# Index columns copied for one or for two ring groups at a time in the plain gather passes of a graph-network kernel

## The chip, the core and the metric

The kernel runs on one core of a Trainium2 chip. The time is the device time of one execution in microseconds (us); before the change it was 10801.46 us, the median of three runs.

## The reference, cut to what matters

A graph of 6250 nodes (256 features each) and 100000 edges, sorted by destination, passes through four layers: `L0` an attention layer with four heads, `L1` a convolution with a weight for each edge, `L2` two convolutions one behind the other, `L3` an attention layer with eight heads. Each is added to the residual stream. What matters here are the three sums over edges of `L1` and `L2`:

```python
# L1
out = segment_sum(w[:, None] * support[col], row, n) + segment_sum(w[:, None] * support[row], col, n)
# L2, twice
msg = x[src] @ W_msg + b_msg
agg = segment_sum(msg, dst, num_segments=n)
return agg + x @ W_self + b_self
```

For each of them the row `table[src]` of 256 floats must be fetched for every edge and added to the row of its destination.

## The kernel before, in words

The edges are padded to 784 tiles of 128 (`ET`). Nodes are kept in 49 tiles of 128 (`NT`). Four edge tiles are a *ring group* (`EG` = 4), so there are 196 groups (`NEG`). Two edge tiles are a pair. One *visit* joins one pair with one node tile; there are 440 visits (`NV`, 392 pairs and 48 for pairs that straddle node tiles), taken in 110 units of four (`VG`, `NU`).

`plain_pass` (L1016) sums the edges of one layer. It is called three times: `l1` (L2205; weighted, with a `fold` that adds eight partial sums of the other direction, which an earlier pass scattered to HBM), `l2a` (L2229) and `l2b` (L2256), the last two with an `own` matrix product for each node tile in between. Within a pass the engines work side by side:

- GpSimd (POOL in the profile) runs `gather` (L1003). For each group it waits for the group's slot in the ring (L1008, L1009; `RG` = 6 slots of four tiles in `rows_in`), copies the group's four index columns out of `gidx` into the slot of `gather_rows` (L998, in `index_columns`), waits for the copy's own semaphore (L999, L1000), and issues four indirect DMAs (L1012), each of which fetches 128 rows of 1 KB. The loop's body is one turn of the ring, six groups; 32 turns run in the loop, and four groups follow it.
- The sync engine (SP) runs `landed_groups` (L967): it waits until the four DMAs of a group have landed and raises `s_landed` (L976); three groups later it gives the slot back (`ring_free`, L984) when `s_add` shows that all visits of that group are done.
- VectorE (DVE) builds one-hot matrices `hot` for the eight half-visits of a unit from `iota` and `rel`: in `l2a` and `l2b` by one instruction of 128x1024 with two inputs (L941), in `l1` by eight small ones (L944). It also adds each visit's result from PSUM to the accumulator (L956).
- TensorE waits for `s_landed` (L1100) and for a free PSUM bank (L1101), and multiplies the one-hots with the fetched rows (L1103), a visit being two products of 128x128 by 128x256. Each fp32 product stands in the trace as two records.
- In `l2a` and `l2b` TensorE also transposes a node tile (L1111) and multiplies it with the layer's own weights (L1119), once in two units; ScalarE copies for it.

`gather` is also called by the two attention layers: `attention_fetch0` (L1256; groups of four, ring of eight) and `attention_fetch3` (L1902; groups of eight tiles, `GS` = 8, ring of six). Between the gathers no engine but GpSimd issues indirect DMAs. `scatter_pass` (L1722) is an earlier phase. The helper `turns` (L63) takes the number of steps and the number of steps in one loop body; a step's `u.c` is a Python number that counts within the body, `u.val` is the edge group's number (in the loop a register expression).

Of the kernel before, what the change touches and what calls it, by code (L numbers as in the profile page):

```python
# [5 lines left out]
I32 = mybir.dt.int32  # L6
# [4 lines left out]
P = 128  # L11
N, D, E = (6250, 256, 100000)
# [3 lines left out]
ET = 784  # L16
# [9 lines left out]
GS = 2 * VG  # L26
EG = 4
NEG = ET // EG
RG, RG0 = (6, 8)
# [33 lines left out]
def turns(eng, total, body, lag, steady=None):  # L63
    first = -(-lag // body) * body
    loops = max(0, ((steady or total) - first) // body)
    if loops < 2:
        first, loops = total + lag, 0
    for v in range(first):
        yield Turn(v, v, total, False)
    if loops:  # L70
        with eng.Fori(0, loops) as i:
            for k in range(body):
                yield Turn(i * body + (first + k), first + k, total, True)
        for v in range(first + loops * body, total + lag):
            yield Turn(v, v, total, False)

def build(nc, t, out):
    with ExitStack() as top:
        made = {}

        def own(name):
            made[name] = made.get(name, 0) + 1
            return name if made[name] == 1 else f'{name}_{made[name]}'

        def sb(name, shape, dt=F32, ctx=top):
            return ctx.enter_context(nc.sbuf_tensor(own(name), shape, dt))

        def bank(name, ctx):
            return ctx.enter_context(nc.psum_tensor(own(name), [P, 512], F32))

        def sem(name):
            return top.enter_context(nc.semaphore(name))
# [18 lines left out]
        gidx = sb('gidx', [P, ET], I32)  # L111
# [13 lines left out]
        def dram(name, shape, dt=F32):  # L125
            return nc.dram_tensor(name, shape, dt).ap()
        T0, T1, T2, T3 = (dram(f'table{i}', [NP, D]) for i in range(4))
        T4 = dram('table4', [NP, WT])
# [15 lines left out]
        own_v, own_a, own_p = (sem(f's_own_{k}') for k in 'vap')  # L144
# [19 lines left out]
        ring_free = [sem(f's_ring_free{b}') for b in range(RG0)]  # L164
# [22 lines left out]
        def phase():  # L187
            return nc.Block()
# [757 lines left out]
        def rows_count(name, n=2):  # L946
            return [Count(sem(f's_rows_{name}{b}')) for b in range(n)]
# [45 lines left out]
                sp.wait_ge(ring_free[b], 1)  # L993
                sp.sem_inc(ring_free[b], -1)

        def index_columns(g, u, ring, per, idx):
            b = u.c % ring
            g.tensor_copy(idx[:, b, :], gidx[:, bass.ds(u.val * per, per)]).then_inc(own_p, 1)  # L998
            g.wait_ge(own_p, 1)  # L999
            g.sem_inc(own_p, -1)  # L1000
            return [idx[:, b, j:j + 1] for j in range(per)]

        def gather(g, table, rows_of, s_rows, ring, per, free, idx):  # L1003
            top_row = g.to_reg(NP - 1)

            def fetch(u):
                b = u.c % ring
                g.wait_ge(free[b], 1)  # L1008
                g.sem_inc(free[b], -1)  # L1009
                rows = index_columns(g, u, ring, per, idx)  # L1010
                for j in range(per):
                    g.indirect_dma_start(out=rows_of(b * per + j), out_offset=None, in_=table, in_offset=bass.IndirectOffsetOnAxis(ap=rows[j], axis=0), bounds_check=top_row, oob_is_err=True).then_inc(s_rows[b].sem, 16)  # L1012
            for t_ in turns(g, ET // per, ring, 0):
                fetch(t_.at(0))

        def plain_pass(name, table, acc, acc_flat, width, weighted, fold=None, own=None):  # L1016
            NB = 4
            s_rows = rows_count(name, RG)
            with ExitStack() as ctx:
                G = sb('rows_in', [P, RG * EG, width], F32, ctx)  # L1020
                idx = sb('gather_rows', [P, RG, EG], I32, ctx)
                hot = sb('hot', [P, 2, GS, P], F32, ctx)
                wgt = sb('step_weights', [P, S], F32, ctx) if weighted else None
                ps = [bank(f'ps_p{i}', ctx) for i in range(NB)]
# [13 lines left out]
                with phase() as block:  # L1038
# [45 lines left out]

                    @block.gpsimd
                    def _(g):
                        gather(g, table, lambda k: G[:, k, 0:D], s_rows, RG, EG, ring_free, idx)

                    @block.tensor
                    def _(te):  # L1090
# [130 lines left out]
        def attention_fetch0(LG, attc, room):  # L1221
            G = part(room, 0, [RG0 * EG, D])
            rows_by = part(room, RG0 * EG * D, [2, GS * P // 2]).bitcast(BF16)
            spread = part(room, RG0 * EG * D + GS * P, [2, GS * P])
            s_rows = rows_count('att0_', RG0)
# [2 lines left out]
            row_free = [sem(f's_row_free{b}') for b in (0, 1)]  # L1228
            with ExitStack() as ctx:
                feat = sb('feat', [P, 2, 2 * D], F32, ctx)  # L1230
                idx = sb('gather_rows', [P, RG0, EG], I32, ctx)
                featT = sb('featT', [P, 2, 4, P], F32, ctx)
                psX = [bank(f'psX{b}', ctx) for b in (0, 1)]
                psF = [bank(f'psF{b}', ctx) for b in (0, 1)]
# [1 line left out]
                with phase() as block:  # L1236
# [16 lines left out]

                    @block.gpsimd
                    def _(g):
                        gather(g, T0, lambda k: G[:, k, :], s_rows, RG0, EG, ring_free, idx)  # L1256

                    @block.scalar
                    def _(a):
# [595 lines left out]
        def attention_fetch3(LG, SV, rows_room, T_room):  # L1855
            R3 = 6
            NG3 = ET // GS
            AHEAD = 13
            G = part(rows_room, 0, [R3 * GS, WT])
            rows_by = part(T_room, 0, [2, GS * P // 2]).bitcast(BF16)  # L1860
            spread = part(T_room, 2 * GS * P, [2, GS * P])
            s_rows = rows_count('att3_', R3)
# [3 lines left out]
            free3 = [sem(f's_slot_free3{b}') for b in range(R3)]  # L1866
            read3 = [sem(f's_slot_read3{b}') for b in range(R3)]
            with ExitStack() as ctx:
                psS = [bank(f'psS{b}', ctx) for b in (0, 1)]
                idx = sb('gather_rows', [P, R3, GS], I32, ctx)  # L1870
                with phase() as block:

                    @block.sync
# [25 lines left out]

                    @block.gpsimd  # L1900
                    def _(g):
                        gather(g, T4, lambda k: G[:, k, :], s_rows, R3, GS, free3, idx)  # L1902

                    @block.scalar
                    def _(a):
# [460 lines left out]
```

## Time and profile before

| what | value |
|---|---|
| median of the three runs | 10801.46 us (10778.44 to 10802.27) |
| time of the profiled execution | 10752.12 us |
| its span in the trace | 10750.4 us |
| TensorE's mean granted clock | 0.739 |
| busy: TensorE matmul, weight load | 6331.9 us (59%), 4941.0 us (46%) |
| busy: VectorE, ScalarE | 5005.6 us (47%), 1331.9 us (12%) |
| busy: GpSimd | 5855.2 us (54%), 5805 instructions |
| software queue of the DMA engines (all gathers and scatters) | 634.04 MB, 26.7% of 16 engines |

The shares are averages over some forty phases with different limits, so they don't say what bounds a plain pass. The three plain passes lie at about 4530 to 5720 us, 5783 to 7030 us and 7142 to 8390 us of the span. "POOLq", "SPq", "PEq" and "DVEq" are the sequencers of the engines, which take instructions in order and hand them to the engine; a line behind the arrow names what an idle engine was waiting for, and "issue" is time in which it waited for nothing that the profile shows.

### The profile page before, as it was taken

Reading aid. Unit: us, or ns where it says so; the run is one execution under the profiler, and the core shown is the slowest. Engines: PE = TensorE matmul, PEld = TensorE weight load, DVE = VectorE, ACT = ScalarE, POOL = GpSimd, SP = SyncE. Lnnn points to the kernel's source line nnn. Section 1 sums busy time; section 2 is a strip of 40 time slices with the busy share of each in tenths; the row PEclk is TensorE's granted clock in tenths of the full one; section 3 lists DMA queues with packets and bytes.
Section 4 is the critical chain, followed back from the end, with each engine's and each line's share of the span. In section 5 each row is a group of like instructions: output and inputs, shape, how many; then the busy total and the mean of one; then the engine's idle time right before and its main releaser. Section 6 shows DMA issues by size and latency. Waiting matters only on the chain. (4 is left out here: it accounts for less than half of the span.)

```text
span 10750.4 us, 137753 instructions
## 1 busy us (share of the span) xinstructions
PE 6331.9 (59%) x24674; PEld 4941.0 (46%) x24675; DVE 5005.6 (47%) x12212; ACT 1331.9 (12%) x3940; POOL 5855.2 (54%) x5805
## 2 busy tenths in 40 slices
PE   4888875757466666555554555555555642222575
PEld 2888864546344444433333444444444442222454
DVE  6555558885444444355553222242222321114888
ACT  2222211213222222100001000010000300000000
POOL 3777740000288888777775777747777167763000
PEclk9898878988777777676766777677777655555798
DMA  4666674541377777644433222222222166663454
GB/s 147 189 190 187 186 231 152 169 136 35 69 104 105 104 104 105 111 134 137 133 117 91 82 82 82 82 75 81 83 83 83 41 193 204 201 193 99 129 170 155
DMA packets 835068, 1358.92 MB, mean 126 GB/s; under 512 B 112279, under 2 KB 488661, under 8 KB 834981
## 3 DMA queue, kind: packets, MB, share of 16 engines
q0 software_dynamic: 315328, 634.04, 26.7%
q1 hardware_dynamic: 385684, 562.46, 16.0%
q10 hardware_dynamic: 133968, 161.50, 4.8%
q8 instruction: 26, 0.43, 0.0%
q14 instruction: 62, 0.50, 0.0%
HBM read 943.05 MB, written 414.50 MB: 126 GB/s over the span
## 5 line engine op out<-in xcount | busy, mean ns | idle before, releaser
L1012 POOL DMA_INDIRECT rows_in<-table,gather_rows x2352 | 2500.5, 1063 | 1034.2 <-issue 511.1
L1103 PE MATMUL ps_p<-rows_in,hot 128*128 x5280 | 2000.5, 542 | 1584.6 <-SPq L976 1328.8
L1103 PEld LDWEIGHTS ps_p<-rows_in,hot 128*128 128x128 f32 x5280 | 1360.3, 271 | 2180.1 <-issue 1928.7
L1722 POOL DMA_INDIRECT scatter_sums<-regionC,idx x880 | 1387.3, 1576 | 307.1 <-issue 246.0
L956 DVE TENSOR_TENSOR regionC<-regionC,ps_p 128x257 f32 (+2 forms) x1320 | 558.6, 423 | 1767.9 <-DVEq L953 1569.1
L1464 PE MATMUL ps_p<-regionA 128*128 128x265 f32 (+1 forms) x3520 | 969.4, 435 | 426.0 <-DVE regionC L956 194.4
L1464 PEld LDWEIGHTS ps_p<-regionA 128*128 128x128 f32 x3520 | 735.3, 214 | 659.8 <-DVE regionC L956 239.3
L1012 POOL DMA_INDIRECT regionB<-table,gather_rows x784 | 848.4, 1082 | 344.5 <-issue 272.2
L1012 POOL DMA_INDIRECT regionC<-table,gather_rows x784 | 817.1, 1042 | 296.7 <-issue 265.1
L1927 PE MATMUL psS<-dst_scores,regionA 128*128 x1760 | 393.4, 362 | 793.7 <-issue 385.4
L1927 PEld LDWEIGHTS psS<-dst_scores,regionA 128*128 128x128 f32 x1760 | 383.7, 330 | 803.4 <-issue 803.4
L1795 PE MATMUL psC<-regionC 128*128 128x128 f32 x1760 | 370.5, 377 | 649.1 <-PEq L1793 647.8
L1807 PE MATMUL psO<-regionA,regionC 128*128 x1760 | 675.1, 552 | 8.8 <-PEq L1806 1.8
L1795 PEld LDWEIGHTS psC<-regionC 128*128 128x128 f32 x1760 | 319.2, 272 | 753.3 <-issue 752.9
L956 DVE TENSOR_TENSOR regionB<-regionB,ps_p 128x265 f32 (+1 forms) x880 | 372.5, 423 | 586.1 <-DVEq L953 472.5
L1537 POOL MEMSET ones<- 128x128 f32 x2 | 0.4, 206 | 1109.1 <-POOLq L2052 940.3
L1807 PEld LDWEIGHTS psO<-regionA,regionC 128*128 128x128 f32 x1760 | 495.1, 295 | 120.7 <-issue 23.8
L1496 DVE TENSOR_TENSOR regionA<-regionA,logits 128x512 f32<-128x512 f32 x880 | 547.6, 684 | 0.0
L1317 PEld LDWEIGHTS psL<-att_cols,featT 128*128 128x128 f32 x3520 | 526.0, 215 | 37.6 <-issue 4.9
L1292 PE MATMUL psX<-regionA,regionB 128*128 x1760 | 528.7, 429 | 21.7 <-PEq L1288 18.6
L1369 DVE TENSOR_TENSOR feat<-regionB,psX 128x512 f32<-128x512 f32 x440 | 301.8, 686 | 499.5 <-DVEq L1368 375.0
L998 POOL COPY gather_rows<-gidx 128x4 int32 (+1 forms) x882 | 221.4, 251 | 468.1 <-POOLq L1009 461.8
(303 smaller groups left out, 8011.7 us busy)
## 6 DMA issues: line engine op xcount, KB each, us to landing
regionA<-edge_rows SPq DMA_DIRECT2D x880, 256.0 KB, 3.2
edge_rows<-regionB SPq DMA_DIRECT2D x196, 512.0 KB
edge_rows<-regionC SPq DMA_DIRECT2D x392, 256.0 KB
regionC<-srcrow_d SPq DMA_DIRECT2D x220, 256.0 KB
scatter_sums<-zero_rows ACTq DMA_DIRECT2D x8, 6400.0 KB, 42.3
regionA<-scatter_sums ACTq DMA_DIRECT2D x49, 1024.0 KB
rows_in<-table,gather_rows POOLq DMA_INDIRECT x2352
regionB<-rrow_d ACTq DMA_DIRECT2D x110, 256.0 KB
```

Source lines behind the costliest of these rows:

```text
L956: v.tensor_tensor(dst_, dst_, ps[(u.c * VG + j) % nbank][:, 0:width], ALU.add).then_inc(s_add.sem, 1)
L1012: g.indirect_dma_start(out=rows_of(b * per + j), out_offset=None, in_=table, in_offset=bass.IndirectOffsetOnAxis(ap=rows[j], axis=0), boun ...
L1103: x = te.matmul(ps[(u.c * VG + j) % NB][:, 0:width], hot[:, b, 2 * j + k, :], at_tile(G, slot[j] * 2 + k), start=k == 0, stop=k == 1)
L1292: x = te.matmul(psX[b][:, k * D:(k + 1) * D], spread[:, ub, at:at + P], at_tile(A256, nt), start=True, stop=True)
L1317: x = te.matmul(psL[gb][:, col:col + HEADS0], featT[:, b, 2 * k + c, :], attc[:, c, :], start=c == 0, stop=c == 1)
L1369: v.tensor_tensor(feat[:, b, :], G[:, bass.ds(slot * 2, 2), :].rearrange('p a c -> p (a c)'), psX[b][:, :], ALU.add).then_inc(own_v, 1)
L1464: x = te.matmul(ps[(u.c * VG + j) % NB][:, 0:width], hot[:, b, 2 * j + k, :], Gs[:, b * GS + 2 * j + k, :], start=k == 0, stop=k == 1)
L1496: v.tensor_tensor(o, i, w, ALU.mult).then_inc(aux_full[b], 1)
L1722: g.indirect_dma_start(out=scat, out_offset=bass.IndirectOffsetOnAxis(ap=idx[:, b, j:j + 1], axis=0), in_=sums[:, b, j, :], in_offset=None ...
L1795: x = te.matmul(psC[b][:, j * P:(j + 1) * P], hot[:, b * Q + j, :], same[:, b * Q + j, :], start=True, stop=True)
L1807: x = te.matmul(psO[2 * b + j // 2][:, j % 2 * D:(j % 2 + 1) * D], pairs[:, b * Q + j, :], at_tile(SUP, nt[j // 2]), start=True, stop=True)
L1927: x = te.matmul(psS[b][:, j * HEADS3:(j + 1) * HEADS3], spread[:, b, j * P:(j + 1) * P], at_tile(SV, nt[j // 2]), start=True, stop=True)
```

## The change

`index_columns` gets a number `together`. With 2, it copies the index columns of two groups (eight columns) at every second group, and nothing at the other; with 1 it does what it did. The plain passes use 2, the attention layers 1. The buffer `gather_rows` of a plain pass grows from 24 to 48 columns, two turns of the ring, and the body of the gather loop from six to twelve groups (16 turns in the loop, four groups behind it). In the attention layers only the buffer's shape is written differently.

```diff
-        def index_columns(g, u, ring, per, idx):
-            b = u.c % ring
-            g.tensor_copy(idx[:, b, :], gidx[:, bass.ds(u.val * per, per)]).then_inc(own_p, 1)
-            g.wait_ge(own_p, 1)
-            g.sem_inc(own_p, -1)
-            return [idx[:, b, j:j + 1] for j in range(per)]
-
-        def gather(g, table, rows_of, s_rows, ring, per, free, idx):
+        def index_columns(g, u, ring, per, idx, together):
+            b, at = (u.c % (together * ring), u.c % together)
+            if at == 0:
+                n = together * per if not isinstance(u.val, int) else min(together * per, ET - u.val * per)
+                g.tensor_copy(idx[:, b * per:b * per + n], gidx[:, bass.ds(u.val * per, n)]).then_inc(own_p, 1)
+                g.wait_ge(own_p, 1)
+                g.sem_inc(own_p, -1)
+            return [idx[:, b * per + j:b * per + j + 1] for j in range(per)]
+
+        def gather(g, table, rows_of, s_rows, ring, per, free, idx, together):
             top_row = g.to_reg(NP - 1)
 
             def fetch(u):
                 b = u.c % ring
                 g.wait_ge(free[b], 1)
                 g.sem_inc(free[b], -1)
-                rows = index_columns(g, u, ring, per, idx)
+                rows = index_columns(g, u, ring, per, idx, together)
...
-            for t_ in turns(g, ET // per, ring, 0):
+            for t_ in turns(g, ET // per, together * ring, 0):
                 fetch(t_.at(0))
...
-                idx = sb('gather_rows', [P, RG, EG], I32, ctx)
+                idx = sb('gather_rows', [P, 2 * RG * EG], I32, ctx)
...
-                        gather(g, table, lambda k: G[:, k, 0:D], s_rows, RG, EG, ring_free, idx)
+                        gather(g, table, lambda k: G[:, k, 0:D], s_rows, RG, EG, ring_free, idx, 2)
...
-                idx = sb('gather_rows', [P, RG0, EG], I32, ctx)
+                idx = sb('gather_rows', [P, RG0 * EG], I32, ctx)
...
-                        gather(g, T0, lambda k: G[:, k, :], s_rows, RG0, EG, ring_free, idx)
+                        gather(g, T0, lambda k: G[:, k, :], s_rows, RG0, EG, ring_free, idx, 1)
...
-                idx = sb('gather_rows', [P, R3, GS], I32, ctx)
+                idx = sb('gather_rows', [P, R3 * GS], I32, ctx)
...
-                        gather(g, T4, lambda k: G[:, k, :], s_rows, R3, GS, free3, idx)
+                        gather(g, T4, lambda k: G[:, k, :], s_rows, R3, GS, free3, idx, 1)
```

## Rows read from the trace of the kernel before

**Rows 1.** The page's costliest groups: busy, mean ns | idle before, releaser.

```profile
L1012 POOL DMA_INDIRECT rows_in<-table,gather_rows x2352 | 2500.5, 1063 | 1034.2 <-issue 511.1
L1103 PE MATMUL ps_p<-rows_in,hot 128*128 x5280 | 2000.5, 542 | 1584.6 <-SPq L976 1328.8
```

**Rows 2.** Waits of the second pass: engine line <- releaser: us, times, longest us.

```profile
PE ps_p L1103 <- SPq L976: 479.4, 174, 4.9
POOL rows_in L1012 <- issue: 157.2, 468, 1.8
POOL rows_in L1012 <- POOLq L1000: 129.0, 162, 0.8
POOL gather_rows L998 <- POOLq L1009: 63.0, 1, 63.0
POOL rows_in L1012 <- POOLq L1009: 39.6, 130, 0.3
```

**Rows 3.** The three passes, busy by engine, granted clock, DMA share, GB/s.

```profile
core 0: us, PE busy (x) PEld busy (x) DVE busy (x) ACT busy (x) POOL busy (x), PEclk, DMA share, GB/s
4530.00:5720.00 1190.00, 676.21 (x1752) 463.28 (x1752) 626.76 (x1416) 0.00 (x0) 842.68 (x980) 0.69 0.43 129
5782.00:7030.00 1248.00, 736.56 (x2046) 518.00 (x2046) 343.68 (x598) 38.64 (x97) 900.86 (x980) 0.72 0.28 82
7142.00:8390.00 1248.00, 729.99 (x2046) 520.03 (x2046) 342.07 (x598) 38.62 (x97) 900.85 (x980) 0.73 0.28 82
```

**Rows 4.** Timeline of GpSimd in the first pass: start, us, what, idle before.

```profile
4594.57 1.01 POOL L1012 DMA_INDIRECT rows_in<-table,gather_rows  x1 [0.30 <-issue]
4595.89 1.01 POOL L1012 DMA_INDIRECT rows_in<-table,gather_rows  x1 [0.30 <-issue]
4596.91 0.19 POOL L998 COPY gather_rows<-gidx 128x4 int32 x1
4597.90 1.04 POOL L1012 DMA_INDIRECT rows_in<-table,gather_rows  x1 [0.79 <-POOL gather_rows L998]
4599.24 1.01 POOL L1012 DMA_INDIRECT rows_in<-table,gather_rows  x1 [0.30 <-issue]
4600.56 1.01 POOL L1012 DMA_INDIRECT rows_in<-table,gather_rows  x1 [0.31 <-issue]
4601.88 1.01 POOL L1012 DMA_INDIRECT rows_in<-table,gather_rows  x1 [0.30 <-issue]
4602.90 0.19 POOL L998 COPY gather_rows<-gidx 128x4 int32 x1
```

**Rows 5.** Timeline of GpSimd in `attention_fetch3`: groups of eight gathers.

```profile
9003.33 1.04 POOL L1012 DMA_INDIRECT regionC<-table,gather_rows  x1 [0.80 <-POOL gather_rows L998]
...
9012.58 1.01 POOL L1012 DMA_INDIRECT regionC<-table,gather_rows  x1 [0.30 <-issue]
9016.88 0.19 POOL L998 COPY gather_rows<-gidx 128x8 int32 x1 [3.28 <-POOLq L1009]
```

**Rows 6.** GpSimd by shape: first pass, then the second.

```profile
L1012 POOL DMA_INDIRECT rows_in<-table,gather_rows x784 | 802.2, 1023 | 345.0 <-issue 191.9 <-POOLq L1000 69.9 <-POOL gather_rows L998 47.6
L998 POOL COPY gather_rows<-gidx 128x4 int32 x192 | 39.8, 207 | 13.4 <-POOLq L1009 12.2
...
L1012 POOL DMA_INDIRECT rows_in<-table,gather_rows x784 | 850.3, 1085 | 345.0 <-issue 157.2 <-POOLq L1000 129.0 <-POOLq L1009 39.6
L998 POOL COPY gather_rows<-gidx 128x4 int32 x192 | 49.9, 260 | 64.1 <-POOLq L1009 63.0
```

**Rows 7.** Timeline of the second pass: a one-hot of VectorE beside the gathers.

```profile
6290.82 1.22 DVE L941 TENSOR_TENSOR hot<-iota,rel 128x1024 f32<-128x1024 f32 x1
6290.96 1.96 POOL L1012 DMA_INDIRECT rows_in<-table,gather_rows  x1 [0.30 <-issue]
...
6304.91 0.20 POOL L998 COPY gather_rows<-gidx 128x4 int32 x1
...
6306.98 3.79 PE L1103 MATMUL ps_p<-rows_in,hot 128*128 x8 [3.94 <-SPq L976]
```

**Rows 8.** VectorE in the second pass by shape: the one-hots.

```profile
L941 DVE TENSOR_TENSOR hot<-iota,rel 128x1024 f32<-128x1024 f32 x110 | 134.5, 1224 | 5.4 <-DVEq L961 0.2
```

**Rows 9.** Timeline of GpSimd: long pauses, two in the first pass, one in `attention_fetch3`.

```profile
4702.68 1.01 POOL L1012 DMA_INDIRECT rows_in<-table,gather_rows  x1 [1.76 <-issue]
4848.68 1.01 POOL L1012 DMA_INDIRECT rows_in<-table,gather_rows  x1 [1.77 <-issue]
...
9148.27 1.07 POOL L1012 DMA_INDIRECT regionC<-table,gather_rows  x1 [1.40 <-issue]
```

## The prediction

> **What bounds the kernel now.** The page's busy shares decide nothing here, so I first read the costliest groups. In the plain passes TensorE's products stand idle for 1584.6 us, 1328.8 of them until the sync engine says that a group of gathered rows has landed (L976) [rows 1]. GpSimd's gathers of the same passes wait mostly for "issue", for nothing another engine does. Next I read the waits of one pass. TensorE waits 174 times for a landing, 479.4 us together; GpSimd waits for a slot of the ring (L1009) once for long, 63.0 us ahead of the pass, and after that never longer than the 0.3 us that lies ahead of every gather [rows 2]. So nobody holds GpSimd up, and it holds up the others. The windows agree: TensorE is busy for 676 of 1190 us in the first pass and for 737 and 730 of 1248 in the others, the DMA engines for 28% to 43% [rows 3]. Last I read GpSimd's timeline: gather behind gather without a hole that belongs to someone else [rows 4]. A plain pass lasts as long as GpSimd needs to issue 784 gathers and 196 copies, and a microsecond saved there is a microsecond of the kernel, three times over.
>
> **The change, part by part.**
>
> *Copies removed.* 196 copies a pass become 98, each for eight columns; over three passes 294 go. What one costs must be read from start to start. Inside a group a gather starts 1.32 us behind the one before (4594.57, 4595.89). Across a copy it is 2.01 us (4595.89 to 4597.90): the gather's 1.01, the copy's 0.19, and then 0.79 in which the next gather can't start, since its sequencer had to wait for the copy's semaphore (L1000) before it could take the gather up [rows 4]. Without the copy the 0.19 and the wait go, and the usual 0.30 stays. The gather behind a copy is also longer itself, 1.04 against 1.01, so the next start comes after 1.34 instead of 1.32 (4597.90, 4599.24). Together 0.69 + 0.02 = 0.71 us for each copy, and 294 x 0.71 = **209 us**. A check: the group's period is 4602.90 - 4596.91 = 5.99 us, and 196 of them are 1174 of the pass's 1190.
>
> By durations alone the sum would be smaller: 294 copies of 0.207 to 0.272 us are some 70 us, and the wait behind them is booked as idle time. The Trainium skill ("Perfetto Trace Analysis", GPSIMD Engine Instruction) advises to time GpSimd by the spacing of starts and calls its spans unreliable; by that rule it is the 209 that counts.
>
> *Is the gap of 0.30 what stays where a group begins without a copy?* There the sequencer still waits for a slot and lowers its semaphore (L1008, L1009). In the trace this work is already hidden: the second gather of a group is put down to L1009 in 130 cases, with 0.3 us at the longest [rows 2], so the sequencer reaches the next group's slot while the present group's first gathers run, some three gathers early. Eight gathers in a row at that pace exist as well: in `attention_fetch3` from 9003.33 to 9012.58, seven spacings, 9.25 us, 1.32 each [rows 5]. The bounds are 0.30 and 0.79 (the gap when the sequencer does stop); I take 0.30.
>
> *The copies that stay are twice as wide.* The eight-column copy takes 0.19 us as the four-column one does [rows 4, 5]. Cost nothing.
>
> *Twice the loop body, twice the buffer.* The body holds 48 gathers instead of 24, and half of the 32 branches of a pass go. `attention_fetch3` runs a loop with 48 gathers in its body at the same spacing [rows 5], so I take nothing; the branch is hidden behind running gathers. The buffer is a few bytes more. The attention layers issue the same instructions as before: nothing.
>
> *One-hots of VectorE against GpSimd.* In the first pass a gather takes 1.023 us on average and a copy 0.207; in the second 1.085 and 0.260 [rows 6]. The excess is 784 x 0.062 + 196 x 0.053 = 59 us a pass. It comes from the 110 one-hots of 1.22 us [rows 8]: a gather that starts under one is held until it ends (1.96 us from 6290.96, under a one-hot from 6290.82) [rows 7]. That is 0.54 us a one-hot. If the starts of gathers fall anywhere under a one-hot, the mean hold is about half its length, 0.6, with copies or without. The same 110 one-hots meet the same 784 gathers afterwards, so I leave the 59 us as they are. The bounds are a hold of 0 and one of 1.22: from 119 us less to 150 us more for both passes. Neither end is near, as the phase of gathers against one-hots wanders with the number of visits in a group; a quarter of it, ±45 us, goes into the range.
>
> Two sentences of the Trainium skill would give something else. By "SBUF — State Buffer" (Who interferes with whom) a VectorE instruction with two SBUF inputs collides with GpSimd instructions that read SBUF, and by "Perfetto Trace Analysis" (DMA Instruction — SWDGE) a DMA that GpSimd issues reads no tensor; only copies would be held, and half of the 59 us would go with half of the copies, 59 more for both passes. The trace doesn't bear the second one out: copies carry only 10 of the 59 us, and a gather itself was held to 1.96 us.
>
> *Do the others keep up?* A group now comes every 5.99 - 0.71/2 = 5.64 us, in the later passes every (1248 - 70)/196, some 6.0. TensorE is busy 737/196 = 3.8 us a group at a mean granted clock of 0.72; all of it at 1.2 GHz would be an estimated 3.8 x 0.72/0.5 = 5.4 us. Even then it keeps up, barely. Slots are given back in time: a group lands about 2 us behind its last gather (6304.91 to 6306.98) [rows 7], the slot behind it is released three groups late, and the ring has six; that leaves more than a group of spare time. What a late slot looks like is seen in `attention_fetch3`, 3.28 us ahead of a copy [rows 5]; the plain passes show none.
>
> *Sum.* -209 us on the path. The profiled execution took 10752.12 us, so its like comes to 10543. It lies 49 us below the median of the runs shown, so against that median: 10801 - 209 = **10592 us**, 1.9% less. A measurement of this kernel can tell about 0.3%, 32 us, from no change.
>
> **The rivals.**
>
> *The sequencer still stops at the group's border.* If the wait for the slot cost what the wait for the copy did, 0.79 would stay and only the copy itself would go: 294 x 0.2 = 59 us, 10742. Against it: the sequencer's lead [rows 2]. Chance 0.03.
>
> *The consumers become the bound.* If TensorE, at the lower clock and with its waits for VectorE's additions, can't take a group in less than about 6.0 us in the stretches with many visits, slots come back late and only half the gain remains: 10697. For it: the estimate of 5.4 lies near 5.64. Against it: in 174 of 196 groups it waited for rows, for 2.8 us each [rows 2]. Chance 0.04.
>
> *It doesn't save what it says.* If landings rather than issues set TensorE's pace, and the DMA engines moved rows no faster for being asked earlier, no change: 10801. Against it: they are busy 28% in the later passes [rows 3]. Chance 0.02.
>
> *Slower: GpSimd's long pauses multiply.* Once in 96 gathers, seven times in the first pass, a gather is preceded by 1.76 us instead of 0.30, with no releaser; in `attention_fetch3` it comes once in 80, at 1.4 [rows 9]. It looks like a store of requests that must be emptied, always ahead of a group's second gather, behind a copy. If the copies' breaks are what lets it empty unseen, half as many breaks could bring a pause with every copy that is left: 294 x 1.46 = 429 us, less the 209: +220, 11021. It decides from 143 pauses more, one in some 14 gathers. Against it: eight gathers in a row bring one in 80, not one in 14. Chance 0.03.
>
> **How the numbers follow.** My forecast has 0.88, with 10592. Its range takes ±45 us for the one-hots, some 20 for the scatter of the medians (24 us between the runs shown) and a little for the gap: 10515 to 10665. The first rival and the consumers' lie above it; they, the third and the slower one are the 0.12 left out. To "faster" go the forecast, the first rival and the second: 0.95. "Same" 0.02, "slower" 0.03.
>
> **What would show it right or wrong.** In the profile after: 294 copies in the plain passes, of eight columns, at about 0.2 us; 588 gaps of 0.79 become 294, and a gather without a copy ahead of it starts 1.32 us behind its neighbour across the group's border; idle time ahead of the gathers falls by 294 x 0.49 = 144 us from 1034.2. The first pass falls from 1190 to 1120 us, the others from 1248 to 1178. TensorE's wait for L976 falls by almost as much as the passes, and POOL's wait for L1009 stays at 0.3. One pause in 80 to 96 gathers remains. It is wrong if a gap of 0.79 stands at borders without a copy, if a wait for L1009 of some microseconds appears ahead of a copy or a gather, or if the passes shorten by much less than GpSimd's saved time.

## The result and the profile after

The changed kernel takes 10647.11 us (median of 4 runs, 10630.78 to 10659.21) against 10797.9 us for the kernel before on the same chip (4 runs, 10778.44 to 10802.27): a ratio of 0.9863 with a 95% interval of 0.9842 to 0.9883, or 151 us less. The forecast was 209 us less, a time of 10592 us with a range of 10515 to 10665. The range holds the result; 0.72 of the gain came. Medians are given with the lowest and highest run or, as a ratio, with their 95% interval; where a kernel ran only once, the text says so.

The profiled execution took 10657.3 us (span 10655.6, mean granted clock 0.738). The lines of the code have moved: the copy is L1000, its wait L1002, the slot's wait L1011, the gather L1014, the product L1105. These are the page's costliest groups again (busy, mean ns | idle before, releaser), the answer to [rows 1]:

```profile
L1014 POOL DMA_INDIRECT rows_in<-table,gather_rows x2352 | 2470.6, 1050 | 944.0 <-issue 693.5
L1105 PE MATMUL ps_p<-rows_in,hot 128*128 x5280 | 1916.0, 524 | 1518.2 <-issue 527.6
```

The idle time ahead of the gathers fell by 90 us (1034.2 to 944.0) where 144 were forecast. Which pass is short of it can be read from the gathers line by line, one row for each pass (durations min/median/max in ns, then the first and the last start). The kernel before:

```profile
L1012 POOL DMA_INDIRECT rows_in<-table,gather_rows x784: 1008/1015/1197, 4531.6 to 5718.5; - x196
L1012 POOL DMA_INDIRECT rows_in<-table,gather_rows x784: 1007/1015/2064, 5783.5 to 7028.4; - x196
L1012 POOL DMA_INDIRECT rows_in<-table,gather_rows x784: 1008/1015/2061, 7143.6 to 8387.9; - x196
L1012 POOL DMA_INDIRECT regionC<-table,gather_rows x784: 1008/1015/1566, 8613.0 to 9791.4; - x196
```

The changed kernel:

```profile
L1014 POOL DMA_INDIRECT rows_in<-table,gather_rows x784: 1006/1012/1194, 4536.9 to 5728.3; - x196
L1014 POOL DMA_INDIRECT rows_in<-table,gather_rows x784: 1006/1012/2085, 5793.6 to 6956.9; - x196
L1014 POOL DMA_INDIRECT rows_in<-table,gather_rows x784: 1006/1012/2067, 7071.7 to 8238.4; - x196
L1014 POOL DMA_INDIRECT regionC<-table,gather_rows x784: 1006/1012/1563, 8463.5 to 9684.8; - x196
```

From first to last start, the second pass went from 1244.9 to 1163.3 us (-81.6) and the third from 1244.3 to 1166.7 (-77.6); 70 each were forecast. The first went from 1186.9 to 1191.4 (+4.5). The three together make -155, close to the 151 between the medians. (The fourth row is `attention_fetch3`, which the change leaves alone. It is 43 us longer in the second of the two profiled executions, most of the reason why their spans differ by only 95.)

On GpSimd's own timeline the change did what it should. Start, us, what, idle before, in the first pass:

```profile
5114.77 1.01 POOL L1014 DMA_INDIRECT rows_in<-table,gather_rows  x1 [0.30 <-issue]
5116.09 1.01 POOL L1014 DMA_INDIRECT rows_in<-table,gather_rows  x1 [0.30 <-issue]
5117.40 1.01 POOL L1014 DMA_INDIRECT rows_in<-table,gather_rows  x1 [0.30 <-issue]
5118.42 0.19 POOL L1000 COPY gather_rows<-gidx 128x8 int32 x1
5119.41 1.04 POOL L1014 DMA_INDIRECT rows_in<-table,gather_rows  x1 [0.79 <-POOL gather_rows L1000]
```

There is no copy between 5108.16 and 5118.42, eight gathers stand 1.32 us apart, and the group's border inside them leaves no mark: the gap there is 0.30. The copy of eight columns takes 0.19, and the 0.79 behind it has stayed, for 98 copies instead of 196. [rows 4] show the same stretch with a copy after every fourth gather.

But in the first pass GpSimd now waits for something else. The waits of the first pass after (engine, line <- releaser: us, times, longest us):

```profile
PE ps_p L1105 <- DVE regionB L956: 262.6, 87, 10.3
PE ps_p L1105 <- SPq L976: 118.2, 16, 48.1
POOL rows_in L1014 <- POOLq L1011: 67.8, 67, 7.3
POOL gather_rows L1000 <- POOLq L1011: 40.7, 10, 12.1
```

And of the same pass before:

```profile
PE ps_p L1103 <- SPq L976: 349.5, 127, 5.6
PE ps_p L1103 <- DVE regionB L956: 22.6, 13, 4.0
POOL rows_in L1012 <- POOLq L1009: 35.7, 117, 0.3
POOL gather_rows L998 <- POOLq L1009: 12.2, 1, 12.2
```

By these rows TensorE no longer waits mostly for rows; it waits for VectorE's additions, 262.6 us instead of 22.6. (How far the split by releaser can be trusted is said behind the experiments.) GpSimd waits for free slots of the ring, up to 7.3 us at a time and 67.8 + 40.7 us together, where the longest wait inside the pass was 0.3. One such place in the changed kernel, all engines, TensorE's weight loads left out:

```profile
5270.94 2.13 DVE L944 TENSOR_SCALAR hot<-iota,rel,step_weights 128x128 f32<-128x128 f32 x8
...
5271.17 2.07 PE L1105 MATMUL ps_p<-rows_in,hot 128*128 x4 [2.36 <-DVE regionB L956]
5272.99 4.01 DVE L1174 TENSOR_REDUCE regionA<-regionA 128x256 f32<-128x2304 f32 x1
5276.92 2.10 DVE L956 TENSOR_TENSOR regionB<-regionB,ps_p 128x256 f32 x4
...
5277.48 2.92 PE L1105 MATMUL ps_p<-rows_in,hot 128*128 x6 [4.24 <-SPq L976]
5278.15 1.01 POOL L1014 DMA_INDIRECT rows_in<-table,gather_rows  x1 [7.33 <-POOLq L1011]
```

VectorE is in the reduction of the sums (4.01 us, L1174) while products finished before wait in the banks. After it four additions run back to back (2.10 us), TensorE starts again, and only then a slot comes free for GpSimd, which has stood for 7.33 us. The kernel before has the same reduction, and its GpSimd never waited over 0.3 us inside the pass. Why does the changed one?

### The profile page after: what moved, and what is told of

Its sections match the earlier page's. It is cut to its first block and busy times, and to the rows that moved or that the text cites. A ratio compares the mean times of both kernels' runs of the same rounds, so it can differ in the third digit from the quotient of the medians.

```text
span 10655.6 us, 136733 instructions
## 1 busy us (share of the span) xinstructions
PE 6231.9 (58%) x24674; PEld 4869.8 (46%) x24675; DVE 5016.8 (47%) x12212; ACT 1330.7 (12%) x3940; POOL 5743.0 (54%) x5511
## 5 line engine op out<-in xcount | busy, mean ns | idle before, releaser
L1014 POOL DMA_INDIRECT rows_in<-table,gather_rows x2352 | 2470.6, 1050 | 944.0 <-issue 693.5
L1105 PE MATMUL ps_p<-rows_in,hot 128*128 x5280 | 1916.0, 524 | 1518.2 <-issue 527.6
L1105 PEld LDWEIGHTS ps_p<-rows_in,hot 128*128 128x128 f32 x5280 | 1312.6, 262 | 2081.5 <-issue 1850.3
L1014 POOL DMA_INDIRECT regionB<-table,gather_rows x784 | 846.1, 1079 | 344.5 <-issue 293.9
L1014 POOL DMA_INDIRECT regionC<-table,gather_rows x784 | 813.0, 1037 | 297.3 <-issue 265.4
L1319 PE MATMUL psL<-att_cols,featT 128*128 128x4 f32 x3520 | 471.4, 257 | 16.6 <-PEq L1312 8.3
```

What stands on the lines that cost most here:

```text
L1105: x = te.matmul(ps[(u.c * VG + j) % NB][:, 0:width], hot[:, b, 2 * j + k, :], at_tile(G, slot[j] * 2 + k), start=k == 0, stop=k == 1)
L1319: x = te.matmul(psL[gb][:, col:col + HEADS0], featT[:, b, 2 * k + c, :], attc[:, c, :], start=c == 0, stop=c == 1)
```

## The experiments

Every kernel here has a mask: the values that TensorE, VectorE and SyncE read from tables and wait for are put through `& 1023` first, which leaves them as they are, since all are smaller. c0_after, c1_after and c2_after are the changed kernel with the mask and nothing else, one for each chip used, and c0_before is the kernel before with it. The mask, its main lines (a third wait, of VectorE in an attention layer, has it too):

```diff
-                                te.wait_ge(s_landed.sem, group[j] + s_landed.base)
+                                te.wait_ge(s_landed.sem, (group[j] & 1023) + s_landed.base)
...
-                done = of_visits(sp, visits_by[0:1, :], u.val, regs, NV)[0]
+                sp.load(regs, visits_by[0:1, bass.ds(u.val, 1)])
+                sp.reg_alu(masked[0], regs[0], 1023, ALU.bitwise_and)
+                done = sp.snap(masked[0], min_val=0, max_val=NV)
```

**The first chip: control, one part undone, two pieces of work made lighter.** e1_fold_single undoes the change in the first plain pass alone:

```diff
-                        gather(g, table, lambda k: G[:, k, 0:D], s_rows, RG, EG, ring_free, idx, 2)
+                        gather(g, table, lambda k: G[:, k, 0:D], s_rows, RG, EG, ring_free, idx, 1 if fold else 2)
```

e2_short_reduce reduces one of the nine partial sums, and e3_small_loads loads one of eight; both leave out part of the sum that the first pass folds in.

```diff
-                                v.tensor_reduce(total, parts[:, b].rearrange('p k c -> p c k'), AX.X, ALU.add).then_inc(own_v, 1)
+                                v.tensor_reduce(total, parts[:, b, 0:1].rearrange('p k c -> p c k'), AX.X, ALU.add).then_inc(own_v, 1)
...
-                                a.dma_start(parts[:, b, 0:CHAINS, :], scat.rearrange('(k n) c -> n k c', k=CHAINS)[bass.ds(u.val * (P // 2), P), :, :]).then_inc(s_load[b].sem, 16)
+                                a.dma_start(parts[:, b, 0:1, :], scat.rearrange('(k n) c -> n k c', k=CHAINS)[bass.ds(u.val * (P // 2), P), 0:1, :]).then_inc(s_load[b].sem, 16)
```

> The changed kernel with one register operation more ahead of three kinds of waits: the value that is loaded from memory is masked with 1023 before it is waited against (L976 to L984 on the sync engine, L1100 on TensorE, the attention layer's wait on VectorE). All experiments below carry these masks, so this run is their control. Both theories: like the changed kernel, 10630 to 10670 us, first plain pass about 1190 us, the second and third about 1165 to 1170 us.

> The first plain pass (the one with the fold) copies index columns for one group again, the other two for two. Theory A (in the first pass something other than GpSimd's issue sets the pace once a group takes less than about 6.05 us, so the 98 copies that are gone there bring nothing): no more than 15 us off the control, the first pass at 1185 to 1195 us. Rival (the first pass did gain and lost it by chance in the profiled execution): about 70 us slower than the control.

> The fold's reduction in the first plain pass reads one of nine partial sums instead of nine (its output leaves the eight scattered sums out); its loads stay. VectorE's 4.0 us become some 0.4, 49 times. Theory B (VectorE's reduction stands in order ahead of the additions that free TensorE's banks, so TensorE and then the ring come late): the first pass falls to about 1120 us, as forecast, and GpSimd waits for slots no more. Theory C (the loads of 1 MB hold the gathers' landings up): the first pass stays at 1180 to 1195 us.

> The fold's loads in the first plain pass fetch one of the eight scattered sums (128 KB instead of 1 MB each); VectorE's reduction stays as long (its output adds seven stale rows). Theory C (the loads hold the landings up): the first pass falls to about 1120 us and a group lands about 2 us behind its last gather throughout. Theory B (VectorE's order): the first pass stays at 1180 to 1195 us, and GpSimd still waits for slots.

On this chip the kernel before took 10715.74 us, 82 less than above. The control took 10486.5 (ratio 0.9779, 0.9763 to 0.9796): 229 us less, more than the forecast. Its gathers of the first pass, and its waits from 4540 to 5640:

```profile
L1017 POOL DMA_INDIRECT rows_in<-table,gather_rows x784: 1009/1015/1245, 4541.2 to 5658.6; - x196
```

```profile
PE ps_p L1108 <- SPq L977: 432.9, 160, 48.2
PE ps_p L1108 <- DVE regionB L956: 40.3, 27, 4.7
PE ps_p L1108 <- issue: 5.8, 18, 0.4
POOL rows_in L1017 <- POOLq L1014: 27.7, 91, 0.3
```

The pass lasts 1117.4 us, 69.5 less than before's 1186.9, and the prediction's two signs hold: GpSimd's wait for slots stays at 0.3, TensorE waits for rows. I had expected the control to repeat the result, 10630 to 10670 us with a first pass of 1190; that fell. e1 took 10550.0 us (0.9848, 0.9831 to 0.9864), and its first pass 1184.7 (4536.0 to 5720.7). Undoing the change in that pass costs 63.5 us of the kernel's time and 67.3 of the pass; by the forecast's working, 98 x 0.71, it is 69.6. So the term for the first pass is right on a chip where nobody else gets in the way, and theory A of e1 (no loss, as nothing was gained) had lost its ground here. e2 took 10484.7 and e3 10479.89 in one run each, with first passes of 1117.4 and 1118.0: the reduction (0.41 us in e2 instead of 4.05) and its loads bind nothing there. That says nothing of the chip of the result, where the first pass isn't GpSimd's; these two missed what they were made for.

**A second chip: is it the mask, and is it VectorE's load?** e5_double_reduce (changed kernel) and e6_before_double_reduce (kernel before) issue the reduction twice. That is 49 x 4.0 = some 196 us more of VectorE's time in the first pass.

```diff
+                                v.tensor_reduce(total, parts[:, b].rearrange('p k c -> p c k'), AX.X, ALU.add).then_inc(own_v, 1)
+                                v.wait_ge(own_v, 1)
+                                v.sem_inc(own_v, -1)
                                 v.tensor_reduce(total, parts[:, b].rearrange('p k c -> p c k'), AX.X, ALU.add).then_inc(own_v, 1)
```

> The kernel before with the same masks as the control. It tells whether the control's gain (0.978 of the kernel before, against 0.986 for the changed kernel itself) is the masks' or the chip's. If the masks cost and bring nothing: equal to the kernel before on the same chip within 0.2%, first pass 1186 to 1189 us. If they bring something (the sync engine's and TensorE's sequencers showed pauses of 0.7 us in the changed kernel and none in the control): some 50 to 80 us faster than the kernel before.

> The control once more, beside the kernel before with masks. Against that one 209 us less are expected from the removed copies (first pass 1118, second and third about 1165).

> The control with the fold's reduction of VectorE done twice in the first pass (4.0 us more, 49 times, 196 us of VectorE's time). Theory (the removed copies took away the consumers' spare time: what was covered when GpSimd needed 6.05 us a group isn't at 5.7): the first pass grows from 1118 to 1150 us or more, and GpSimd waits for slots (L1011) by several microseconds. Rival (VectorE still has spare time, and the changed kernel's first pass lost its gain for another reason): the first pass stays within 10 us of 1118.

> The kernel before (with masks) with the same doubled reduction. Theory: it ends at the same length as the changed kernel with the doubled reduction, as then both are set by the consumers, so the change brings nothing in that pass; it grows by less from its 1188 us. Rival: 1188 us, unchanged, and 70 us above the other.

Here the kernel before took 10791.29 us. c0_before took 10797.21 (1.0004, 0.9995 to 1.0014), so the mask costs nothing. c1_after took 10666.09 (0.9886, 0.9870 to 0.9903), with a first pass of 1183.3 us where 1118 was expected: the loss is back with the very text that had all of the gain on the first chip. Its waits from 4540 to 5700:

```profile
PE ps_p L1108 <- issue: 276.2, 127, 8.2
PE ps_p L1108 <- DVE regionB L956: 189.1, 65, 8.4
POOL rows_in L1017 <- POOLq L1014: 55.0, 57, 6.5
POOL gather_rows L1003 <- POOLq L1014: 21.3, 9, 3.9
```

So what varies is the chip (or its session), and the changed kernel feels it where the kernel before doesn't. The pair e5 and e6, one run each, shows how differently. Their gathers of the first pass, e5 and then e6:

```profile
L1017 POOL DMA_INDIRECT rows_in<-table,gather_rows x784: 1006/1012/1263, 4527.2 to 5758.0; - x196
```

```profile
L1015 POOL DMA_INDIRECT rows_in<-table,gather_rows x784: 1006/1012/1207, 4533.3 to 5717.3; - x196
```

With the doubled reduction the kernel before still needs 1184.0 us, as without it (1186.2 in c0_before), and its GpSimd never waits over 0.3 us for a slot. The changed kernel grows from 1183.3 to 1230.8 and ends 46.8 us longer in this pass than the old one with the same extra work. Had the consumers simply run out of capacity, both would have ended at the same length. I had expected that of e6, and it fell. With the faster supply something else happens.

A trace of it stands in the rows of the sequencers, which the page doesn't count as busy. This is one line (L170, the load of the visits' table entries) on TensorE's sequencer, from 4550 to 5640, min/median/max ns. The kernel before, the changed kernel, c0_after, c1_after, e6, each in its own fence:

```profile
L170 PEldq TENSOR_LOAD <-visits x202: 326/332/345, 4558.0 to 5638.8; - x101
```

```profile
L170 PEldq TENSOR_LOAD <-visits x198: 3/333/727, 4552.8 to 5623.3; - x198
```

```profile
L170 PEldq TENSOR_LOAD <-visits x214: 326/332/346, 4558.0 to 5634.7; - x107
```

```profile
L170 PEldq TENSOR_LOAD <-visits x200: 3/332/1393, 4554.9 to 5633.9; - x100
```

```profile
L170 PEldq TENSOR_LOAD <-visits x202: 326/332/346, 4559.6 to 5637.8; - x101
```

Where the pass keeps its gain (c0_after) or never had one (before, e6), every one of these loads takes 0.33 us. Where the gain is lost, some last 0.7 us and one 1.4, and others are recorded as 3 ns, as if they had been put on record behind a stop. VectorE's sequencer shows the same (344 ns at the median, 365 at most before, 729 after), and so do its plain register operations (69 ns at most before, 727 after). I call them the sequencers' pauses. They don't by themselves cost a pass its gain. The changed kernel's second pass, which gained 81.6 us, has them on TensorE's sequencer too (5800 to 6900), while VectorE's has none there (354 ns at most):

```profile
L170 PEldq TENSOR_LOAD <-visits x208: 4/332/700, 5809.4 to 6898.2; - x104
```

Nor are they new with the change: in `attention_fetch3` the kernel before has loads of up to 1.2 us on TensorE's sequencer and 1.4 on VectorE's, and SyncE's has one operation of 0.6 us in its first pass.

**A third chip: the loop's length or the supply?** Two causes were left. The change doubles the body of GpSimd's loop, and it makes the supply faster. e7_long_body has the long body with a copy for every group; e8_short_body has the short body with a copy for two groups and a buffer of one turn.

```diff
 e7_long_body
-            b, at = (u.c % (together * ring), u.c % together)
+            b, at = (u.c % (together * ring), 0)
...
-                n = together * per if not isinstance(u.val, int) else min(together * per, ET - u.val * per)
+                n = per
 e8_short_body
-            b, at = (u.c % (together * ring), u.c % together)
+            b, at = (u.c % ring, u.c % together)
...
-            for t_ in turns(g, ET // per, together * ring, 0):
+            for t_ in turns(g, ET // per, ring, 0):
...
-                idx = sb('gather_rows', [P, 2 * RG * EG], I32, ctx)
+                idx = sb('gather_rows', [P, RG * EG], I32, ctx)
```

> The control once more. On a chip where the kernel before takes some 10795 us: about 10650, first pass 1184 to 1192 us, with pauses of 0.7 us in the sequencers of TensorE, VectorE and the sync engine in the plain passes. On one where the kernel before takes some 10716: about 10487, first pass 1118 us, no such pauses.

> Index columns copied for one group at a time as before, but the gather loop's body stays at twelve groups. Theory D (the longer loop body of GpSimd brings the 0.7 us pauses of the other sequencers, through the fetching of instructions): pauses in the first plain pass as in the control, and the passes no faster than before, 1188, 1246, 1246 us. Theory E (the pauses come with the faster supply, when the consumers' sequencers have no idle time left in which to run ahead): no pauses of TensorE and VectorE there, passes 1188, 1246, 1246 us.

> Index columns copied for two groups at a time, with the old loop body of six groups and the old buffer of one turn. Theory D: no pauses, and the first pass falls to about 1120 us on either chip, 70 us less than the control where the kernel before takes 10795. Theory E: the pauses are there as in the control, and the first pass stays at 1184 to 1192 us on such a chip.

The kernel before took 10767.5 us here, c2_after 10569.6 in one run, with a first pass of 1173.3, which is neither of the two cases expected of it. e7 took 10766.42 in one run, its first pass 1184.2 and its second and third 1243.4 and 1244.0: the old time in every pass, within 3 us of the kernel before on the chip of the result. e8 took 10588.16 (0.9835, 0.9817 to 0.9852), with a first pass of 1163.3, between theory D's 1120 and theory E's 1184 to 1192, but with the pauses of theory E. L170 on TensorE's sequencer once more, e7 and then e8:

```profile
L170 PEldq TENSOR_LOAD <-visits x204: 328/332/346, 4550.1 to 5637.9; - x102
```

```profile
L170 PEldq TENSOR_LOAD <-visits x202: 3/332/714, 4556.9 to 5624.2; - x101
```

The long body brings neither a gain nor, on TensorE and VectorE, pauses; fewer copies bring both. The loop's length is acquitted, and with it the larger buffer and the halved branches: the whole effect of the change, good and bad, is that of the copies left out.

**A fourth chip: more room between TensorE and VectorE.** If it were only VectorE's long reduction that holds TensorE up, eight banks in place of four should take up the shock.

```diff
-            NB = 4
+            NB = 8 if fold else 4
```

> The control with eight PSUM banks instead of four in the first plain pass, so that TensorE may be eight visits ahead of VectorE's additions instead of four; nothing else changes. Theory (on chips with pauses the first pass is held by TensorE and VectorE waiting for one another over four banks, 247.8 us of TensorE's waits for L956 in the changed kernel's first pass against 22.6 before): TensorE's wait for L956 falls to some 20 us and the first pass to between 1120 and 1150 us also where the kernel before takes 10765 us or more; the whole some 30 to 60 us below the control of such a chip (10646 to 10675 where the kernel before takes 10791). Rival (the pauses themselves, in every sequencer, take the time, and more banks only shift the waiting to the landings): the first pass stays at 1174 to 1192 us there. Where the kernel before takes some 10716 both expect 1118 us.

The kernel before took 10763.86 us, e4 10587.19 (0.9837, 0.9820 to 0.9853). Its waits of the first pass:

```profile
PE ps_p L1108 <- issue: 301.5, 139, 12.4
PE ps_p L1108 <- PEq L1103: 103.9, 24, 8.3
PE ps_p L1108 <- DVE regionB L956: 62.1, 25, 5.4
POOL rows_in L1017 <- POOLq L1014: 46.6, 60, 7.5
POOL gather_rows L1003 <- POOLq L1014: 34.1, 8, 12.2
```

TensorE's wait for the additions fell to 62.1 us (about 173 to 192 in the controls of the second and third chips), yet the pass lasts 1164.9 us, and GpSimd waits for slots as long as before. That is outside both expectations (1120 to 1150, 1174 to 1192). It is no measure of the banks either: the control didn't run on this chip, and c2_after and e8, with the same supply and four banks, are already 10 us apart (1173.3 and 1163.3). The waiting has changed its name: 103.9 us now stand behind L1103, where TensorE has waited for VectorE's one-hots (5.5 in c2_after). It still waits for VectorE, whose program builds a unit's one-hots, then reduces, then adds the unit before. So eight banks alone don't free it, and VectorE isn't cleared as the one that holds it up.

## Why the prediction was right, and where it wasn't

*What a copy costs.* 0.71 us from start to start, of which 0.79 - 0.30 is idle time. Right, and shown by taking the copies away and putting them back (e1, e7, e8). The second and third passes give 81.6 and 77.6 us for 98 copies, 0.83 and 0.79 a copy; with idle time ahead of the gathers falling from 345.0 [rows 6] and, in the third pass, 344.3 to 297.4 and 300.2, which is 48 and 44 of the forecast 98 x 0.49 = 48. On the first chip the first pass gives 67.3 to 69.5 for 69.6.

*The border without a copy.* 0.30 was taken between 0.30 and 0.79, and 0.30 is what the timeline shows. The rival with the stopping sequencer is out.

*Width, body, buffer.* The eight-column copies average 0.199 us in the first pass (0.207 for the narrow ones before), and e7 (one run) and e8 show no price of the body's length.

*One-hots against GpSimd.* The 59 us of extra durations were left as they are, with ±45 in the range. That was called a quarter of the span from 119 less to 150 more; a quarter is 34. In the second pass the gathers' mean is 1067 ns (1085 before) and the copies' 278 (260), one row each by shape:

```profile
L1014 POOL DMA_INDIRECT rows_in<-table,gather_rows x784 | 836.5, 1067 | 297.4 <-issue 229.9 <-POOL gather_rows L1000 25.4 <-POOLq L1002 21.4
L1000 POOL COPY gather_rows<-gidx 128x8 int32 x96 | 26.6, 278 | 66.8 <-POOLq L1011 66.4
```

Against 850.3 and 49.9 us before, that is 37 us less busy time in this pass: 23 from the copies left out (49.9 to 26.6) and 14 from gathers that were held less. Those 14 are about the surplus of 12 over the forecast 70: 49 gathers of this pass took over 1.3 us, 65 before. In c0_after 66 did, so it varies from run to run. By the Trainium skill ("Perfetto Trace Analysis", DMA Instruction — SWDGE) such a DMA reads no tensor. Joined with the prediction's other sentence of the skill, by which VectorE holds up what GpSimd reads, no gather would be held; the trace disagrees after the change as well, with a longest gather of 2085 ns in this pass against a median of 1012.

*Long pauses of GpSimd.* Right: the first four stand at 4704.95, 4855.61, 4999.69 and 5145.38, with 1.77 us each, 96 gathers apart, as at 4702.68 and 4848.68 before [rows 9]. The slower rival is out; with half the copies the queue behaves as it did.

*Do the others keep up?* **This is the step that failed**, in the first pass alone, and by the prediction's own sign: "a wait for L1009 of some microseconds". The prediction put a group at 5.64 us, TensorE's need at 5.4 at worst, and "more than a group of spare time" in the slots, and so booked the full 70 us. What came was +4.5 on the chip of the result, where "POOL's wait for L1009 stays at 0.3" became 7.3. On the other chips that show pauses the first pass gave 3 us (second), 11 (third; 21 in e8's form) and, with eight banks, about 20. The prediction's conditions for this rival were right in kind (waits of TensorE for VectorE's additions, late slots) but it was placed in stretches at the lower clock, worth half of the whole gain, at 0.04. The clock isn't the cause: the mean granted clock of the first pass is 0.68 after and 0.69 before [rows 3], and TensorE's busy time there, between 4536 and 5730 us, is no longer than it was:

```profile
core 0: us, PE busy (x) PEld busy (x) DVE busy (x) ACT busy (x) POOL busy (x), PEclk, DMA share, GB/s
4536.00:5730.00 1194.00, 628.55 (x1748) 441.99 (x1748) 636.08 (x1412) 0.00 (x0) 817.34 (x882) 0.68 0.43 129
```

The clock is a little lower in c1_after, c2_after and e8 (0.66 to 0.67) than in c0_after (0.70), but a record of a product is as long (376 ns of busy time in c1_after, 378 in c0_after).

What the working left out is that the work isn't even: VectorE does 49 reductions of 4 us in this pass, each of which stops the additions, and averages of 3.8 or 5.4 us a group don't show them. The later passes have no such reduction. There TensorE waits for VectorE's additions too (100.1 us in the second pass, 5.8 before), but GpSimd waits for a slot, but for the start, no longer than 3.0 us in the second and 3.2 in the third. The reductions alone don't explain the loss, though: c0_after has them all and waits no longer than 0.3 us for a slot, and e2, with each cut to 0.41 us, is no faster there. They count where the pauses are: doubled, they cost the changed kernel 47.5 us on the second chip (1183.3 to 1230.8). What a shorter reduction brings on such a chip was not run.

*The sum.* -81.6 - 77.6 + 4.5 = -155, the medians say -151. The forecast's -209 was missed by the 74 us of the first pass, less 19 that the others gave beyond it. That the time still lies in the range is luck: the range was made of ±45 us for the one-hots and 20 for scatter, and nothing in it stood for a pass that pays out nothing. With the second chip's ratio, 0.9886, the kernel would have come to 10678 us, outside it.

**What is shown and what isn't.** Shown: the gain per copy; that the first pass gives it fully on one of the chips, nearly not at all on two, and 11 to 21 of 70 us on two more; that mask and loop length have no part in it; that in the plain passes the pauses on TensorE and VectorE come with the faster supply and in no kernel with the old one (before, c0_before, e6, e7); that VectorE's plain load doesn't explain it (e6 against e5). Not shown: that the pauses are what delays the slots. SyncE hands a slot back in the order of its program, by a wait for the additions (L983) that stands ahead of its next announcement of landed rows (L976), so one late addition also holds back rows that have landed; nothing was run on that. Open: what makes the pauses.

The recording itself is the strongest rival, and it is untested. Every timed run here was recorded, and the records are not alike. The first pass of c0_after left 15879 semaphore updates in its trace, that of c1_after, the same kernel, 4796; the kernel before left 10657 and 9725 (c0_before), the changed one 4686. The instructions' own records are equal in number, 139277 in both controls. So the traces of every session with pauses lack a large part of these records, most with the faster supply, while the first chip's, without pauses in the plain passes, hold three times as many. Pauses, the records lost and the loss of the gain go together; whether the recording makes all three, or something on the chip makes them, only runs without it could tell. It also makes the split of the waits rough, since a wait is given to a releaser by these records: 276.2 us of TensorE's idle time in c1_after go to "issue", 5.8 in c0_after. The lengths of the passes and of GpSimd's idle stretches, up to 7.33 us, come from the instructions' own records and don't hang on that.

None of the versions beats the changed kernel by more than the chips differ. e8 is about as fast (0.9835, and 0.9837 with e4's eight banks, against 0.9816 for c2_after's one run) with half the buffer and the loop as it was, which makes it the simpler form of the same change.

## What to carry to other kernels

Cost a small instruction on GpSimd by the spacing of starts with and without it, not by its own duration: a copy of 0.2 us was worth 0.7, since its semaphore made the sequencer stop. Before booking such a gain in full, look in each stage for single long operations of the engine that gives the buffers back, here 4 us; the mean load doesn't show them. Here they did no harm on one chip and went with the loss on others, so they mark the stage to doubt and don't decide it. Give such a gain per stage, measure it in more than one session, and before explaining a difference between two traces of one kernel, see whether both hold the same number of records.

## What was not expected of the hardware

The same kernel before took 10716, 10798, 10791, 10767 and 10764 us in the five sessions here, 0.8% apart, while its runs within a session lay 0.22% to 0.24% apart (0.43% in the one with thirteen). `attention_fetch3`, which the change doesn't touch, lasted 1142.0 us in c0_after and 1215.1 in c1_after, from first to last gather, and 1214.5 in c0_before.

The traces of the slower sessions hold fewer semaphore updates than those of the fastest one, of the same kernel, 4796 against 15879 in one pass, and fewer still where GpSimd issues faster.

On the slower chips register operations and table loads of a sequencer, 0.03 to 0.34 us otherwise, sometimes take 0.7 or 1.4 us, at changing places of the loop. (In `attention_fetch3` even c0_after's loads on TensorE's sequencer last 1.0 us at the median, where the kernel before's last 0.33 us.) In the first pass the rows of L170 above show none for c0_after, and up to 1.4 us for c1_after, with the same instructions. In the plain passes they appeared on TensorE only in the kernels whose GpSimd issues gathers faster, although that engine's own instructions were the same. GpSimd's own long pause counts gathers and not time: in the second pass, 6.6% shorter, the first two again stood 96 gathers apart, in 145.0 us instead of 154.6.
